# Causal masks, a bias and the hop scores brought into the score banks by 64x64 products

## The chip, the core and the metric

The kernel runs on one core of a Trainium2 chip. The metric is the device time of one execution in microseconds. A core has TensorE (PE, matrix products), VectorE (DVE), ScalarE (ACT), POOL and SyncE (SP, which issues DMA transfers). Each engine works through its own instructions in order, and semaphores tie them together. TensorE writes only to PSUM, which has banks of 512 fp32 columns on 128 partitions.

## The reference

Two decoder layers on x of 128 sequences x 64 positions x 128 features, each step with a residual and a LayerNorm behind it. Cut to the four attentions that the change touches and the places of the others:

```python
# layer 0
# attention: 16 heads of 8, causal; its output goes through a convolution
# that gives q2, and a second causal attention runs with q2 and the same k, v
scores = jnp.where(tril, einsum('bthd,bshd->bhts', q, k) * scale, -inf)   # twice
# "xattn": mLSTM with hop embeddings, 8 heads of 16
pe = rpe[hops].reshape(S, S, NH, DH)
k_hop = einsum('bhvc,vmhc->bhvm', qh, pe)
C = (einsum('bhsd,bhtd->bhst', qh, k_scaled) + k_hop) * D
# "ffn": rotary causal attention, 16 heads of 8, then 8 experts, top 2
scores = jnp.where(tril, einsum('bqhd,bkhd->bhqk', q, k) / sqrt(hd), -1e9)
# layer 1
# attention: rotary, grouped keys, causal
scores = jnp.where(tril, einsum('bshd,bthd->bhst', q, k) * scale, -inf)
# xattn: the last attention, with a bias per sequence
scores = einsum('bhnd,bhmd->bhnm', qh * scale, kh) + attn_bias[:, None] + attention_mask[:, None]
# ffn: 16 experts, top 2
```

## The kernel before, in words

A tile is two sequences of 64 positions, so 128 rows, and there are NT = 64 tiles. Five loops run over them or over expert slots. Each engine has its own program for each loop, with the order inside a period written out by hand; a period works on several tiles at different steps, and `live` cuts off those that don't exist at the ends. Waits are made by `after(engine, signals...)` and `wait_ge`.

- The first loop (lines around 800 to 842 on TensorE) has the first attention, its convolution and the second attention of layer 0. `scores1(0, i + 1, ...)` and `scores1(1, i - 1, ...)` write the scores of a tile for both.
- Then the hop table is made: k_hop for all sequences goes to DRAM (`hop_dram`), one row per sequence and position with 8 heads x 64 columns.
- The third loop (TensorE up to line 1016) has the mLSTM and the attention of the "ffn". Its order on TensorE ends with the hop scores (lines 1003 to 1016), its mask is `causal5(1)` followed at once by `scores5`.
- The experts of layer 0 follow; then the loop with both attentions of layer 1 (TensorE lines 1061 to 1139): `a5[0]` is the rotary one, with `causal5(0)` well ahead of its scores, and `a5[1]` the last one, with `bias5(1, fm[u])` ahead of its scores. `fm` is the sum of fside and mask, made by POOL (line 2104).
- The second routing, experts and final LayerNorm follow.

The scores of a tile for 16 heads fill two PSUM banks, `scores_ps[:, a, g, :]` with g = 0, 1 for the heads of a half. `a` picks the pair of banks. What is to be added to the scores (mask, bias, hop scores) is put in first by a product with the identity and start=True, and the scores are added to it with start=False. The product with the identity uses all 128 rows and columns of the array, the scores themselves 64x64 quarters: rows 64g for the heads' features, columns 64b for the sequence b. Softmax goes on with VectorE (`row_max`, then `probs` = scores less row_max, in halves), ScalarE (exp into probs), TensorE (`turn_half`, `turn5`: transposes), ScalarE (copy to `turned`), TensorE (`weigh`), VectorE (`recip`, `ctx_o`), TensorE (`turn_ctx`). POOL spreads the keys into a block form (`k_bd`, `shared`, both by a helper) and takes the power of -1/2 for the LayerNorms.

SyncE loads, in `load_hops`, the hop rows of a tile by one transfer into `hop_in`, and in `load_side` a tile of the context, of fside and of the mask by one transfer each. `c_loaded` counts them, 16 per transfer, and the waits on it are worked out from a count of 24 per tile.

Of the kernel before, what the change touches and what calls it, by code (L numbers as in the profile page):

```python
# [29 lines left out]
ALU = mybir.AluOpType  # L30
# [70 lines left out]
def build(nc, T, out):  # L101
# [6 lines left out]
    with ExitStack() as ctx:  # L108
# [141 lines left out]
        fm_in, fm = both("fm_in", 2 * S), both("fm", S)  # L250
# [202 lines left out]
        X4_LOADS, SIDE_LOADS = RING + PUT_LOADS + 16 * NT, RING + PUT_LOADS + 24 * NT  # L453
# [46 lines left out]
        def _(sp):  # L500
# [71 lines left out]
            def load_hops(n, u):  # L572
# [5 lines left out]
                sp.dma_start(hop_in[u], tile_rows(hop_dram, n)).then_inc(c_loaded[u], 16)  # L578
# [146 lines left out]
        def _(pe):  # L725
# [84 lines left out]
            def period(i, j):  # L810
# [12 lines left out]
                if live(i - 1):  # L823
                    after(pe, (q2_copied, i), (tr_copied[1], 2 * i - 2))
                    scores1(1, i - 1, q_T[1], (j - 1) % UN)
# [10 lines left out]
                if live(i + 1):  # L836
                    after(pe, (q1_copied, i + 2), (s["k_copied"], 2 * i + 4 + 4), (tr_copied[0], 2 * i + 2))
# [43 lines left out]
            def causal5(a):  # L881
                for g in range(NR):
                    pe.matmul(scores_ps[:, a, g, :], ident16, causal16.unsqueeze(1).broadcast_to([P, 8, S]),
                              start=True, stop=False, skip_group_check=True)

            def bias5(a, bias):
                for g in range(NR):
                    pe.matmul(scores_ps[:, a, g, :], ident, bias.unsqueeze(1).broadcast_to([P, 8, S]),
                              start=True, stop=False, skip_group_check=True)
# [41 lines left out]
            def period(i, j):  # L931
# [44 lines left out]
                if live(i - 1):  # L976
                    after(pe, a3.copied.of(i - 2))
                    causal5(1)
# [24 lines left out]
                if live(i + 2):  # L1003
                    after(pe, m_copied.of(i + 1), m_shift.of(i + 1), (c_loaded[u], RING + 24 * (i + 2 - u) + 48))
# [1185 lines left out]
```

## Time and profile before

| | us |
|---|---|
| median of 3 runs | 3979.63 |
| lowest, highest | 3977.45, 3980.4 |
| span of the profiled execution | 4030.4 |

The profile is of one execution; its span runs from the first to the last instruction, and is what the rows below refer to. Its views give, in microseconds, busy time by engine, waits by the instruction that waited and the one that released it, and the instructions in order of time.
### The profile page before, as it was taken

To read this page: it belongs to the slowest core of one execution; us is meant where nothing else is said; L and a number is where in the kernel's file an instruction comes from. 1 tells how busy PE (TensorE), PEld (TensorE's weight loads), DVE (VectorE), ACT (ScalarE), POOL (GpSimd) and SP (SyncE) were. 2 spreads that over 40 slices of the span, in tenths; PEclk is the share of its full clock that TensorE was granted. 3 is DMA by queue.
4 is the path that set the end of the run, shared out by engine and by line. 5 is a ranking of instruction groups with operands and counts; after the bars stand their busy time and mean duration, and the time that the engine had idled before them with its cause. 6 is when DMAs were issued, how large, how long until landed. Compare 5 with 4: busy or idle time off the path is not lost.

```text
span 4030.4 us, 92744 instructions
## 1 busy us (share of the span) xinstructions
PE 2840.4 (70%) x28014; PEld 1934.9 (48%) x28017; DVE 2454.1 (61%) x6828; ACT 1588.4 (39%) x3994; POOL 1864.3 (46%) x2306
## 2 busy tenths in 40 slices
PE   3999999758888888881068879999999920266600
PEld 2666666435555555551046656666666610255500
DVE  2777777528888887883011158888888860255445
ACT  2666666324555554540023335555555510011100
POOL 4222222006666666664720046666666617411177
PEclk9999999978999988985589989999999965699855
DMA  2111111351111111111222211111111102111133
GB/s 51 41 41 39 38 41 43 119 167 43 53 48 48 48 48 43 50 28 45 73 77 69 67 32 31 27 28 29 29 27 27 25 15 78 60 55 56 51 83 85
DMA packets 282376, 207.13 MB, mean 51 GB/s; under 512 B 61730, under 2 KB 246455, under 8 KB 281904
## 3 DMA queue, kind: packets, MB, share of 16 engines
q1 hardware_dynamic: 262960, 164.88, 13.9%
q0 software_dynamic: 19200, 39.62, 3.5%
q8 instruction: 105, 1.72, 0.2%
q14 instruction: 111, 0.91, 0.1%
HBM read 114.99 MB, written 90.18 MB: 51 GB/s over the span
## 4 chain that ended last, share of the span: by engine, by line
issue 22%; PE 14%; POOL 11%; DVE 5%; SPq 1%; DMA 0%; POOLq 0%; ACT 0%; DVEq 0%; another core or an unknown queue 0%; ACTq 0%
PE scores_ps L1047 3%; POOL k_bd L1999 2%; POOL shared L1999 2%; POOL got L2096 2%; POOL rows L2051 2%; PE heads_ps L1054 1%; PE desk_ps L1054 1%; PE scores_ps L1165 1%; POOL shared L2150 1%; POOL norm_rstd L1995 1%; PE scores_ps L1167 1%; PE heads_ps L1165 1%; PE desk_ps L1165 1%; DVE e_T L1819 1%; DVE row_max L1573 1%
## 5 line engine op out<-in xcount | busy, mean ns | idle before, releaser
L1995 POOL TENSOR_TENSOR norm_rstd<-norm_veps,minus_half 128x1 f32<-128x1 f32 x384 | 218.0, 568 | 386.3 <-DVE norm_veps L1555 380.6
L2051 POOL DMA_INDIRECT rows<-e_in,slot_put x256 | 249.1, 973 | 164.1 <-issue 107.4
L1276 ACT ACTIVATE probs<-probs 128x512 f32<-128x512 f32 x384 | 240.1, 625 | 132.2 <-DVE probs L1575 131.9
L1573 DVE TENSOR_REDUCE row_max<-scores_ps 128x8 f32<-128x512 f32 x384 | 262.1, 683 | 24.6 <-issue 14.1
L1280 ACT ACTIVATE turned<-scores_ps 128x512 f32<-128x512 f32 x384 | 228.4, 595 | 118.0 <-PE scores_ps L905 112.1
L1575 DVE TENSOR_TENSOR probs<-scores_ps,row_max 128x512 f32<-128x512 f32 x384 | 265.6, 692 | 13.3
L905 PE MATMUL scores_ps<-consts,probs 128*128 128x128 f32 x1536 | 243.7, 282 | 7.7 <-ACT probs L1276 6.8
L1208 ACT ACTIVATE probs<-probs 128x512 f32<-128x512 f32 x256 | 161.3, 630 | 136.1 <-DVE probs L1494 133.8
L1492 DVE TENSOR_REDUCE row_max<-scores_ps 128x8 f32<-128x512 f32 x256 | 174.9, 683 | 62.8 <-PE scores_ps L756 58.1
L2140 POOL TENSOR_TENSOR o_rstd<-o_veps,minus_half 128x2 f32<-128x2 f32 x72 | 50.0, 694 | 293.8 <-DVE o_veps L1924 284.1
L905 PEld LDWEIGHTS scores_ps<-consts,probs 128*128 128x128 f32 x1536 | 176.6, 144 | 16.6 <-ACT probs L1276 10.1
L1494 DVE TENSOR_TENSOR probs<-scores_ps,row_max 128x512 f32<-128x512 f32 x256 | 177.0, 691 | 8.8
L1987 POOL TENSOR_TENSOR shared<-k_raw,consts 128x1024 f32<-128x1024 f32 x32 | 60.7, 1898 | 241.3 <-issue 225.5
L1157 PE MATMUL turned_ps<-consts,shared 128*128 128x128 f32 x144 | 31.3, 304 | 196.3 <-issue 196.3
L1212 ACT ACTIVATE turned<-scores_ps 128x512 f32<-128x512 f32 x256 | 144.8, 596 | 61.3 <-PE scores_ps L765 61.3
L1987 POOL TENSOR_TENSOR k_bd<-k_raw,consts 128x1024 f32<-128x1024 f32 x32 | 60.7, 1898 | 232.5 <-issue 226.1
L1364 ACT ACTIVATE shared<-scores_ps,e_b 128x512 f32<-128x512 f32 x128 | 88.0, 687 | 197.3 <-PE scores_ps L1047 194.3
L1438 ACT ACTIVATE shared<-scores_ps,o_b,o_g 128x128 f32<-128x128 f32 x144 | 58.2, 454 | 269.7 <-PE scores_ps L1182 269.7
L765 PE MATMUL scores_ps<-consts,probs 128*128 128x128 f32 x1024 | 151.4, 280 | 15.9 <-ACT probs L1208 15.9
L2096 POOL DMA_INDIRECT got<-moe,got_at x128 | 127.7, 998 | 72.1 <-POOL got_at L2092 50.8
L1047 PE MATMUL scores_ps<-e_T,e_w 128*128 128x512 f32 x256 | 123.2, 626 | 42.9 <-DVE e_T L1819 41.9
L772 PE MATMUL turned_ps<-v_bd,turned 128*64 128x18 f32 x4096 | 144.8, 214 | 10.6 <-ACT turned L1212 2.7
(337 smaller groups left out, 8322.3 us busy)
## 6 DMA issues: line engine op xcount, KB each, us to landing
hop_dram<-shared SPq DMA_DIRECT2D x64, 256.0 KB, 2.1
hop_in<-hop_dram SPq DMA_DIRECT2D x64, 256.0 KB
rows<-zero_rows SPq DMA_DIRECT2D x64, 144.0 KB
shared<-rows SPq DMA_DIRECT2D x72, 128.0 KB
moe<-shared SPq DMA_DIRECT2D x72, 128.0 KB, 1.8
rows<-zero_rows SPq DMA_DIRECT2D x64, 128.0 KB
c_in<-in_ctx SPq DMA_DIRECT2D x128, 64.0 KB
c_two<-in_ctx SPq DMA_DIRECT2D x128, 64.0 KB
```

The costliest lines, as they stand in the source:

```text
L905: last = pe.transpose(scores_ps[:, a, g, P * k:P * k + P], probs[a][:, P * hp:P * hp + P], ident)
L1047: pe.matmul(scores_ps[:, f // 2, f % 2, 0:GS], e_w1[w][:, P * f:P * f + P], e_T[u], start=True, stop=True).then_inc(up_done, 1)
L1208: act.activation(half, half, ACT.Exp, scale=SCALE).then_inc(exp_ready[a], 1)
L1276: act.activation(half, half, ACT.Exp, scale=scale).then_inc(at.exped.sem, 1)
L1280: act.activation(turned[a][:, 512 * g:512 * g + 512], scores_ps[:, a, g, :], ACT.Identity)\
L1492: dve.tensor_reduce(best, sc, AX, ALU.max).then_inc(sub_ready[a], 1)
L1494: dve.tensor_tensor(probs[a][:, 512 * g:512 * g + 512].rearrange("p (h t) -> p h t", t=S), sc, best.unsqueeze(2).broadcast_to([P, 8, S]), ...
L1573: dve.tensor_reduce(best, sc, AX, ALU.max).then_inc(at.shift.sem, 1)
L1575: dve.tensor_tensor(probs[a][:, 512 * g:512 * g + 512].rearrange("p (h t) -> p h t", t=S), sc, best.unsqueeze(2).broadcast_to([P, 8, S]), ...
L1995: pool.tensor_tensor(n_rstd[:, k, u, :], n_veps[:, k, u, :], minus_half[:, 0:1], ALU.pow).then_inc(sig.sem, 1)
L2051: pool.indirect_dma_start(out=rows, out_offset=bass.IndirectOffsetOnAxis(ap=slot_put[:, c, U * n + i:U * n + i + 1], axis=0), in_=put_rows ...
L2096: pool.indirect_dma_start(out=got[u][:, D * k:D * k + D], out_offset=None, in_=moe0, in_offset=bass.IndirectOffsetOnAxis(ap=got_at[u][:, k ...
```

## The change

Mask, bias and hop scores now go in by 64x64 products too, one for each of the four quarters (g, b). Quarter g reads its rows of the identity and of the added values, so both halves of the partitions must hold the values of both sequences by query position: the mask constant already does, and the other two are loaded to suit. `hop_in` is loaded by two transfers (one for each half of the heads; rows of 64 positions, the two sequences side by side), and fside and mask are each loaded twice, once to either half of the partitions, so `fm_in` and `fm` are twice as wide and POOL adds 128 columns instead of 64. A tile now counts 32 on `c_loaded` for the hop loads and 40 for the side loads, and the constants of the waits follow. A wait on `zeroed` (reached early in the kernel) stands ahead of the quarters.

```diff
@@ buffers and counts
-        fm_in, fm = both("fm_in", 2 * S), both("fm", S)
+        fm_in, fm = both("fm_in", 2 * NB * S), both("fm", NB * S)
-        X4_LOADS, SIDE_LOADS = RING + PUT_LOADS + 16 * NT, RING + PUT_LOADS + 24 * NT
+        HOP_LOADS, FM_LOADS = 32, 40
+        X4_LOADS, SIDE_LOADS = RING + PUT_LOADS + 16 * NT, RING + PUT_LOADS + HOP_LOADS * NT
@@ SyncE, load_hops and load_side
-                sp.dma_start(hop_in[u], tile_rows(hop_dram, n)).then_inc(c_loaded[u], 16)
+                halves = tile_rows(hop_dram, n).rearrange("(b v) (g k) -> g v b k", b=NB, g=NR)
+                for g in range(NR):
+                    sp.dma_start(hop_in[u][64 * g:64 * g + 64].rearrange("p (b k) -> p b k", b=NB), halves[g])\
+                      .then_inc(c_loaded[u], 16)
-                sp.dma_start(fm_in[u][:, 0:S], tile_rows(fs_flat, n)).then_inc(c_loaded[u], 16)
-                sp.dma_start(fm_in[u][:, S:2 * S], tile_rows(mask_flat, n)).then_inc(c_loaded[u], 16)
+                for k, rows in enumerate((fs_flat, mask_flat)):
+                    by_query = tile_rows(rows, n).rearrange("(b v) m -> v b m", b=NB)
+                    for g in range(NR):
+                        sp.dma_start(fm_in[u][64 * g:64 * g + 64, P * k:P * k + P].rearrange("p (b m) -> p b m", b=NB), by_query)\
+                          .then_inc(c_loaded[u], 16)
@@ TensorE
+            def mask_quarters(a):
+                for g in range(NR):
+                    rows = slice(64 * g, 64 * g + 64)
+                    for b in range(NB):
+                        pe.matmul(scores_ps[S * b:S * b + S, a, g, :], ident16[rows, rows],
+                                  causal16[rows].unsqueeze(1).broadcast_to([64, 8, S]), start=True, stop=False,
+                                  skip_group_check=True)
             def scores1(a, n, q, k):
-                for g in range(NR):
-                    pe.matmul(scores_ps[:, a, g, :], ident16, causal16.unsqueeze(1).broadcast_to([P, 8, S]),
-                              start=True, stop=False, skip_group_check=True)
+                mask_quarters(a)
...
             def bias5(a, bias):
                 for g in range(NR):
-                    pe.matmul(scores_ps[:, a, g, :], ident, bias.unsqueeze(1).broadcast_to([P, 8, S]),
-                              start=True, stop=False, skip_group_check=True)
+                    rows = slice(64 * g, 64 * g + 64)
+                    for b in range(NB):
+                        pe.matmul(scores_ps[S * b:S * b + S, a, g, :], ident[rows, rows],
+                                  bias[rows, S * b:S * b + S].unsqueeze(1).broadcast_to([64, 8, S]),
+                                  start=True, stop=False, skip_group_check=True)
...
                     for g in range(NR):
-                        pe.matmul(scores_ps[:, 0, g, 0:256], ident, hop_in[u][:, 256 * g:256 * g + 256], start=True, stop=False,
-                                  skip_group_check=True)
+                        rows = slice(64 * g, 64 * g + 64)
+                        for b in range(NB):
+                            pe.matmul(scores_ps[S * b:S * b + S, 0, g, 0:256], ident[rows, rows],
+                                      hop_in[u][rows, 256 * b:256 * b + 256], start=True, stop=False, skip_group_check=True)
@@ POOL
-                    pool.tensor_tensor(fm[1 - u], fm_in[1 - u][:, 0:S], fm_in[1 - u][:, S:2 * S], ALU.add)\
+                    pool.tensor_tensor(fm[1 - u], fm_in[1 - u][:, 0:P], fm_in[1 - u][:, P:2 * P], ALU.add)\
                         .then_inc(fm_added.sem, 1)
```

`causal5` is gone; `mask_quarters` takes its place in both later loops.

## Rows read from the trace of the kernel before

**Rows 1.** The page: busy time (share of the span) and instructions by engine.

```profile
PE 2840.4 (70%) x28014; PEld 1934.9 (48%) x28017; DVE 2454.1 (61%) x6828; ACT 1588.4 (39%) x3994; POOL 1864.3 (46%) x2306
```

**Rows 2.** Windows: stretch, us; busy of PE, PEld, DVE, ACT, POOL; PEclk, DMA, GB/s.

```profile
60.00:720.00 660.00, 619.61 (x7720) 410.27 (x7720) 462.70 (x1059) 421.91 (x1007) 177.89 (x188) 0.99 0.13 39
...
1294.60:1307.70 13.10, 11.14 (x118) 7.35 (x118) 11.93 (x41) 6.53 (x18) 9.45 (x13) 1.00 0.20 53
1307.70:1322.30 14.60, 12.63 (x118) 7.63 (x117) 12.86 (x42) 8.15 (x21) 10.86 (x14) 0.88 0.16 48
...
1317.00:1320.40 3.40, 3.40 (x13) 0.95 (x14) 2.63 (x10) 2.18 (x5) 1.08 (x2) 0.53 0.20 57
...
2701.10:2715.00 13.90, 12.91 (x147) 9.03 (x147) 12.04 (x30) 7.75 (x21) 9.05 (x13) 1.00 0.11 28
```

**Rows 3.** Waits of TensorE, 60 to 720: total us, times, longest.

```profile
PE turned_ps L780 <- DVE ctx_o L1503: 14.5, 60, 0.3
```

**Rows 4.** Timeline of TensorE, stage 1: start, us, instruction, [idle before <- releaser].

```profile
299.91 0.59 PE L750 MATMUL scores_ps<-consts 128*128 128x512 bf16 x2
...
300.12 0.38 PE L750 MATMUL scores_ps<-consts 128*128 128x512 bf16 x1
...
300.43 1.09 PE L756 MATMUL scores_ps<-shared,q_ring 64*64 64x512 f32 x8
301.45 0.66 PE L765 MATMUL scores_ps<-consts,probs 128*128 128x128 f32 x4
...
307.78 0.33 PE L780 MATMUL turned_ps<-consts,ctx_o 128*128 128x128 f32 x1 [0.23 <-DVE ctx_o L1503]
...
310.25 0.59 PE L750 MATMUL scores_ps<-consts 128*128 128x512 bf16 x2
```

**Rows 5.** Timeline of VectorE in stage 1, and a hand-off to it at 78.74.

```profile
301.36 0.15 DVE L1478 TENSOR_SCALAR veps<-mv 128x1 f32<-128x1 f32 x1
301.59 0.69 DVE L1492 TENSOR_REDUCE row_max<-scores_ps 128x8 f32<-128x512 f32 x1
302.32 0.69 DVE L1494 TENSOR_TENSOR probs<-scores_ps,row_max 128x512 f32<-128x512 f32 x1
302.93 0.68 DVE L1492 TENSOR_REDUCE row_max<-scores_ps 128x8 f32<-128x512 f32 x1
...
78.74 1.09 PE L756 MATMUL scores_ps<-k_bd,q_T 64*64 64x512 f32 x8
...
79.90 0.69 DVE L1492 TENSOR_REDUCE row_max<-scores_ps 128x8 f32<-128x512 f32 x1 [3.27 <-PE scores_ps L756]
```

**Rows 6.** Timeline of VectorE, where its chain comes back from POOL.

```profile
306.83 0.40 DVE L1482 TENSOR_SCALAR x_out<-y,mv,rstd 128x128 f32<-128x128 f32 x1 [2.50 <-POOL rstd L1975]
```

**Rows 7.** Waits of VectorE, 985 to 1800.

```profile
DVE rope_c L1581 <- PE heads_ps L936: 24.0, 20, 3.2
```

**Rows 8.** Timeline of a long period in stage 2 and the start of the next.

```profile
1307.68 1.03 PE L1006 MATMUL scores_ps<-hop_in,consts 128*128 128x256 f32 x4
...
1308.64 0.66 PE L1013 MATMUL scores_ps<-k_bd,e_T 64*64 64x256 f32 x8
1309.24 1.16 PE L936 MATMUL heads_ps<-h_T,ffn_attn_w 128*128 128x128 f32 x8
...
1316.99 1.03 PE L883 MATMUL scores_ps<-consts 128*128 128x512 bf16 x2 [0.69 <-ACT turned L1280]
...
1325.05 0.42 DVE L1581 TENSOR_TENSOR rope_c<-heads_ps,consts 128x256 f32<-128x256 f32 x1 [0.88 <-PE heads_ps L936]
```

**Rows 9.** Timeline of TensorE in stage 3.

```profile
2701.11 1.94 PE L888 MATMUL scores_ps<-fm,consts 128*128 128x512 f32 x4
2702.89 0.39 PE L1083 MATMUL desk_ps<-h_T,c_w 128*128 128x128 f32 x2
...
2708.96 0.33 PE L1118 MATMUL heads_ps<-consts,g_diag 128*128 128x128 f32 x1 [0.60 <-DVE g_diag L1559]
```

**Rows 10.** Timeline of POOL and of SyncE's issues in stage 3.

```profile
2704.82 0.31 POOL L2104 TENSOR_TENSOR fm<-fm_in 128x64 f32<-128x64 f32 x1
...
2707.07 0.38 SPq L658 DMA_DIRECT2D fm_in<-in_mask_BxSxS_ff  x1
```

More of the change, by code:

```diff
@@ L823, in period @@
                 if live(i - 1):
-                    after(pe, (q2_copied, i), (tr_copied[1], 2 * i - 2))
+                    after(pe, (zeroed, U + 1), (q2_copied, i), (tr_copied[1], 2 * i - 2))
                     scores1(1, i - 1, q_T[1], (j - 1) % UN)
@@ L836, in period @@
                 if live(i + 1):
-                    after(pe, (q1_copied, i + 2), (s["k_copied"], 2 * i + 4 + 4), (tr_copied[0], 2 * i + 2))
+                    after(pe, (zeroed, U + 1), (q1_copied, i + 2), (s["k_copied"], 2 * i + 4 + 4), (tr_copied[0], 2 * i + 2))
                     scores1(0, i + 1, q_ring[:, 1 - u, :], (j + 1) % UN)
@@ L976, in period @@
                 if live(i - 1):
-                    after(pe, a3.copied.of(i - 2))
-                    causal5(1)
+                    after(pe, (zeroed, U + 1), a3.copied.of(i - 2))
+                    mask_quarters(1)
                     after(pe, (zeroed, U + 1), f_spread.of(i - 1))
@@ L1079, in period @@
                 if live(i):
-                    after(pe, fm_added.of(i), a5[1].copied.of(i - 1))
+                    after(pe, (zeroed, U + 1), fm_added.of(i), a5[1].copied.of(i - 1))
                     bias5(1, fm[u])
@@ L1097, in period @@
                 if live(i + 1):
[L1098 removed]
+                    after(pe, (c_loaded[1 - u], SIDE_LOADS + FM_LOADS * (i + 1 - (1 - u)) + 2 * FM_LOADS), b_q_copied.of(i), a_v_copied.of(i + 2), b_v_copied.of(i))
                     pe.transpose(desk_ps[:, P:2 * P], c_in[1 - u], ident).then_inc(c_turned.sem, 1)
@@ L1105, in period @@
                 if live(i + 2):
-                    after(pe, a5[0].copied.of(i + 1))
-                    causal5(0)
+                    after(pe, (zeroed, U + 1), a5[0].copied.of(i + 1))
+                    mask_quarters(0)
                 if live(i - 2):
@@ L1310, in period @@
                 if live(i + 1):
-                    after(act, m_weighed.of(i - 1), (c_loaded[1 - u], RING + 24 * (i + 1 - (1 - u)) + 48))
+                    after(act, m_weighed.of(i - 1), (c_loaded[1 - u], RING + HOP_LOADS * (i + 1 - (1 - u)) + 2 * HOP_LOADS))
                     mvv = m_vbd[1 - u].rearrange("p (g b h c) -> p g b h c", g=4, b=NB, h=2)
@@ L2102, in period @@
                 if live(i + 1):
-                    after(pool, (c_loaded[1 - u], SIDE_LOADS + 24 * (i + 1 - (1 - u)) + 48), a5[1].score.of(i - 1))
-                    pool.tensor_tensor(fm[1 - u], fm_in[1 - u][:, 0:S], fm_in[1 - u][:, S:2 * S], ALU.add)\
+                    after(pool, (c_loaded[1 - u], SIDE_LOADS + FM_LOADS * (i + 1 - (1 - u)) + 2 * FM_LOADS), a5[1].score.of(i - 1))
+                    pool.tensor_tensor(fm[1 - u], fm_in[1 - u][:, 0:P], fm_in[1 - u][:, P:2 * P], ALU.add)\
                         .then_inc(fm_added.sem, 1)
```

11 lines of the change are left out of this document (3 added, 8 removed).

## Prediction

> **What bounds the kernel now.** I read the page's first two parts first. TensorE is busy 70% of the span, more than any other engine [rows 1], and a change that shortens TensorE's work looks welcome. The share says nothing about who waits, so I then took the windows by stage. The edits lie in three stages, each a loop over the 64 tiles: the first two attentions (about 60 to 720 us), the hop attention with the third softmax attention (985 to 1800), and the last two attentions (2430 to 3200). TensorE is busy 94%, 85% to 87% and 93% of them; VectorE is busy 70% in the first, 91% in an ordinary period of the second, and 87% in the third [rows 2]. I call these stage 1, 2 and 3. A steady period is 10.34 us in stage 1, from one first mask to the next (299.91 to 310.25 [rows 4]), 13.1 in stage 2 and 13.9 in stage 3 [rows 2].
>
> In stage 1 the waits view shows TensorE idle in every period, 0.24 us for VectorE's ctx_o (60 times) [rows 3], and a second time for ScalarE's probs. An engine that waits in each period doesn't set the period alone; the question for each masked score is what stands right behind it. The stage has two masks per tile.
>
> The mask of the first attention starts at 299.91, its scores at 300.43, and the four quarters of the scores run to 301.45 [rows 4]. VectorE's row_max on them starts at 301.59. The instruction before it ended at 301.51, so the two seem to follow closely, but VectorE overlaps neighbours that don't depend on each other by 0.08: the row_max at 302.93 starts before the probs of 302.32 ends at 303.01 [rows 5]. This row_max could have started at 301.43. It waits 0.16 us for TensorE, and no wait is listed since the gap is so short. The row of 79.90, where VectorE had been idle for 3.27 us, confirms it: there row_max comes 1.16 us after the start of the scores (78.74), here too (300.43 to 301.59) [rows 5]. From this row_max a closed chain goes on: VectorE, ScalarE's exp and k_raw, POOL's k_bd and rstd, VectorE's x_out at 306.83 [rows 6], ctx_o, the other attention's row_max and probs, and ScalarE's exp, which TensorE awaits with the next first mask right behind it. So the first mask is on the path for 0.16 us.
>
> The mask of the second attention isn't. Its scores are finished when VectorE is still held up by POOL's rstd (it waits 2.50 us for it), and TensorE itself waits 0.23 at 307.78 for the ctx_o that follows [rows 4, 6].
>
> In stage 2 an ordinary period is VectorE's. It is busy 11.93 of 13.10 us in small instructions with gaps between, and its regular wait is one for POOL's norm_rstd, not for TensorE [rows 2]. But some periods are long: 14.6 us with a mean granted clock of 0.88, among neighbours of 13.1 at 1.00. In them the stretch at 1317 is at 0.53 [rows 2], so TensorE's clock is at its lower level of 1.2 GHz; ahead of it TensorE had had waits, the last of them 0.69 us, and mostly short products. The mask group then takes 1.03 us, against 0.59 for the same in stage 1 [rows 4, 8], and in the next period VectorE's rope_c waits 0.88 us for L936 [rows 8]. The waits view has 24.0 us of that kind in 20 places [rows 7]. There TensorE's work is on the path.
>
> In stage 3 TensorE waits 0.60 us for the g_diag that VectorE writes [rows 9]. From there the path is TensorE's, L1118 to L1131 in the listing, with VectorE waiting for it at both LayerNorm and rope, and then VectorE's again, with one copy in it that lasts until POOL's k_bd ends. Neither the bias (L888, 2701.11 [rows 9]) nor this stage's mask (L883) lies between L1118 and L1131.
>
> **The change part by part.**
>
> Masks, 256 in all (128 in stage 1, 64 each in stages 2 and 3). Two 128x512 bf16 products become four of 64x64 weights. The second product starts 0.21 us after the first, and the scores 0.31 after that [rows 4]: 0.10 of the 0.31 is the step from 128x128 to 64x64. The scores show that four quarters overlap: eight instructions of 512 fp32 columns take 1.02 us where one after the other would take four times 0.46 and more. So a mask of quarters, one 512-column product's 0.21 for each g with the two b side by side, takes 0.10 + 0.21 up to the second g, and with my allowance of 0.04 for what does not overlap quite, 0.35 in all, for 0.52: it saves 0.17. Bounds: 0.21 if the step is free, and a loss of 0.42 (0.10 + 4 x 0.21 - 0.52) if nothing overlaps. I take 0.17, from the nearest row, L756. In stage 1 the first mask pays the smaller of 0.17 and the room of 0.16: 61 steady periods x 0.16 = 9.8 us. The second mask pays nothing; TensorE's wait at L780 grows from 0.23 to 0.4, and the cover is POOL's and VectorE's chain.
>
> Hop scores, 64 pairs. Two 256-column fp32 products take 0.96 us (1307.68 to 1308.64); the quarters behind them with as many columns take 0.60 (L1013) [rows 8]. The step between the tilings is moved ahead, not added, so I take 0.54 and a saving of 0.42 (bounds 0.36 and 0.5). With the mask that is 0.59 us of TensorE per period in stage 2, in ordinary periods all of it cover for nothing. In long ones the wait of rope_c shrinks by 0.59, and by 0.17 more for a mask at the lower clock. If there stay as many, 20 x 0.6 to 0.75 is 12 to 15 us. But TensorE gets emptier in these periods too, and a low clock came after its emptiest part; the periods can meet it more often, each time at a lower price. The other end is therefore no gain. I take the middle, 6 us.
>
> Bias, 64 pairs of 512 fp32 columns: 2701.11 to 2702.89 is 1.78 us [rows 9]; quarters take 1.02 [rows 4] and one step in, 0.10, so 0.66 to 0.76 is saved. It is all in front of the wait at L1118, which grows from 0.60 to about 1.3 us. Worth nothing on the path; the stage's mask too, which sits between unlike tilings and saves at most 0.1. What is late next is g_diag, as before.
>
> A rule speaks against the change here. The two tilings cost 0.10 us at one change [rows 4]; the Trainium skill (TensorEngine Tiling (Array Packing), Tiling Modes, Key Properties) says that changing the tiling mode drains the array. In stages 1 and 2 the number of changes stays, in stage 3 bias and mask each get into and out of 64x64 between 128-row products. By the rule the stage's saving falls from 0.7 to 0.5; both disappear in the same wait.
>
> Loads and POOL. The hop load becomes two and the side loads five instead of three, with about 0.38 us of SyncE's queue each [rows 10]. Behind them are the loads of other tiles a period ahead and one store; with five transfers of 0.38 SyncE's queue has 1.9 of 13.9 us filled, and the tile is used a period later. The sum of fm grows from 64 to 128 columns; 64 take 0.31 [rows 10], 128 at most twice that, and POOL then waits for VectorE anyway: nothing. The extra wait on zeroed is met from the start and is issued while earlier products run: nothing to 0.05 per mask.
>
> Sum: 9.8 + 6 = 16 us. The profiled execution spans 4030.4 us and the median of the runs is 3979.63, so the profile is 1.3% slower than what is timed; the terms are per period and I carry them over as they are: 3979.6 - 16 = 3964.
>
> **The rivals.** (a) Nothing on the path: VectorE's own chain follows within 0.16 us in stage 1, and if the quarters save less than I read, or the low-clock stretches of stage 2 eat up their part, the result is within 8 us of 3979. For it: the margin is a tenth of a microsecond. Against: the hand-off of 1.16 us at 79.90 and 300.43. (b) Slower: the clock. With less in front, TensorE's wait ahead of L1118 [rows 9] doubles, and L1118 to L1131 behind it is all on the path. If the clock falls there as it does in stage 2, each fall costs about 1.5 us, as a long period of stage 2 does (14.6 less 13.1 [rows 2]). It decides above 16 falls in the 61 periods (16 x 1.5 is the forecast's 16 us and 8 more); one in three, as in stage 2, is 20 x 1.5 = 30 us, or 3994. Against: this stage runs at 1.00 throughout today, at 93% busy. The Trainium skill (TensorE: Matmul & The Clock Gate, Why this matters for your kernels) warns that gaps between bursts of products bring the low clock back. (c) Everything TensorE saves is paid: 128 x 0.17 + 64 x 0.59 + 64 x 0.75 = 107 us, 3873. Against: the waits of [rows 3, 9]. If stage 1 pays both masks and stage 2 its 15 us, it is about 3945. (d) The quarters don't overlap when they stream one constant: the masks lose 0.42 and the bias 1.7 us; stage 1 loses 61 x 0.42 = 26, stage 3 what its wait of 0.60 doesn't cover, 61 x 1.1 = 67, so about 4070. Against: the scores, same tiles.
>
> **How the numbers follow.** Forecast (3952 to 3971) 0.50; more gain, around 3945, 0.10, and (c) 0.02; (a) 0.23; (b) 0.12; (d) 0.03. Low 3940 leaves out (c) and some more; high 3991 leaves out (d) and the larger half of (b). A measurement of this kernel can tell about 0.2% (8 us) from no change. Faster by more: the forecast, the larger gains: 0.60. Within: 0.26. Slower: (b), (d): 0.14.
>
> **What would show it.** The period of stage 1 falls from 10.34 to 10.18, with the gap before the first row_max gone and TensorE's waits at L780 and L765 longer. The mask group takes 0.35 up to the scores. In stage 2 ordinary periods stay at 13.1 and long ones come down to about 13.9; their number shows whether the clock takes back the rest. In stage 3 the period stays at 13.9 with the wait at L1118 near 1.3 us and the clock at 1.00; if it is below 1.00 there, rival (b) is at work. The prediction is wrong in kind if stage 3 gets shorter: then the bias was on a path that I didn't see.

## The result, and the profile after

The changed kernel took 3995.2 us (median of 20 runs, 3984.2 to 4009.6) against 3980.5 us for the kernel before (20 runs): a ratio of 1.0033, 95% interval 1.0023 to 1.0043, so 13 us slower (9 to 17). The forecast was 3964, 16 us faster.

The page of the changed kernel, against [rows 1]: TensorE has 78 us less work, and every other engine the same or a little more.

```profile
PE 2762.1 (69%) x29038; PEld 1911.3 (48%) x29041; DVE 2457.5 (62%) x6828; ACT 1588.8 (40%) x3994; POOL 1871.8 (47%) x2306
```

The span of this profile, 3988.1 us, is shorter than the 4030.4 of the profile that the prediction read. To tell whether the change or the one profile is odd, the kernel before was profiled again (run before2, below). Its span was 3983.8, and its stages are the yardstick from here on. Windows of the three stages in before2 (stretch, us; busy of PE, PEld, DVE, ACT, POOL; PEclk, DMA, GB/s):

```profile
60.00:720.00 660.00, 621.19 (x7720) 411.92 (x7720) 462.89 (x1059) 421.86 (x1006) 177.53 (x188) 1.00 0.13 39
985.00:1800.00 815.00, 688.47 (x6618) 438.48 (x6616) 676.89 (x2202) 411.64 (x1076) 533.11 (x681) 0.93 0.16 46
2430.00:3200.00 770.00, 740.29 (x8382) 517.06 (x8381) 684.00 (x1656) 444.70 (x1205) 515.56 (x682) 1.00 0.11 29
```

The same windows in the changed kernel:

```profile
60.00:720.00 660.00, 598.05 (x8062) 416.79 (x8063) 463.76 (x1072) 424.75 (x1013) 178.59 (x190) 0.99 0.13 39
985.00:1800.00 815.00, 665.24 (x6971) 444.70 (x6970) 677.66 (x2193) 406.81 (x1067) 530.77 (x679) 0.89 0.16 46
2430.00:3200.00 770.00, 702.05 (x8544) 475.82 (x8545) 678.31 (x1626) 436.50 (x1183) 513.27 (x670) 0.99 0.13 33
```

What is to be seen: TensorE's granted clock went from 0.93 to 0.89 in stage 2 and is below 1.00 in stage 3. What the windows can't show are the lengths of the stages. I take them between the same VectorE instructions in every trace (VectorE has as many in each kernel), from the one that starts nearest 60 us in the profile shown of before to that nearest 720, and so on:

| profile | stage 1 | stage 2 | stage 3 | period of stages 1, 3 |
|---|---|---|---|---|
| before, the profile shown | 657.5 | 815.5 | 770.6 | 10.34, 13.90 |
| before2 | 657.9 | 816.0 | 742.4 | 10.34, 13.39 |
| the changed kernel | 649.9 | 813.4 | 757.9 | 10.20, 13.53 |

Stage 1 does what was forecast (two of its periods, of 11.47 us, are at a lower clock; masks1, below, has none and 647.7 us). Its mask and scores in the changed kernel, and VectorE behind them, against [rows 4, 5]:

```profile
295.46 0.41 PE L760 MATMUL scores_ps<-consts 64*64 64x512 bf16 x4
295.70 1.03 PE L770 MATMUL scores_ps<-shared,q_ring 64*64 64x512 f32 x8
...
296.81 0.15 DVE L1492 TENSOR_SCALAR veps<-mv 128x1 f32<-128x1 f32 x1
296.91 0.69 DVE L1506 TENSOR_REDUCE row_max<-scores_ps 128x8 f32<-128x512 f32 x1
```

The scores come 0.24 us after the mask instead of 0.52, and row_max starts 0.10 after the start of the veps before it, where it had been 0.23 (301.36, 301.59): VectorE no longer waits for TensorE there.

Stage 3 against before2: the period is 0.14 us longer, and five periods are longer still (four of 15.09 us, one near the end of 16.9 for 14.9). The cause of the 0.14 us is in these rows. POOL and VectorE in before2:

```profile
2702.50 1.89 POOL L1999 TENSOR_TENSOR k_bd<-rope_k,consts 128x1024 f32<-128x1024 f32 x1
2704.35 0.32 POOL L2104 TENSOR_TENSOR fm<-fm_in 128x64 f32<-128x64 f32 x1
...
2704.45 0.36 DVE L1849 SCALAR_TENSOR_TENSOR h_mid<-got,got_w,x_in 128x128 f32<-128x128 f32 x1
```

and in the changed kernel:

```profile
2628.65 1.89 POOL L2013 TENSOR_TENSOR k_bd<-rope_k,consts 128x1024 f32<-128x1024 f32 x1
2630.50 0.46 POOL L2118 TENSOR_TENSOR fm<-fm_in 128x128 f32<-128x128 f32 x1
...
2630.60 0.51 DVE L1863 SCALAR_TENSOR_TENSOR h_mid<-got,got_w,x_in 128x128 f32<-128x128 f32 x1
```

VectorE's h_mid starts 0.10 us into POOL's sum of fm and ends 0.14 after it (2704.81 for 2704.67), and with the wider sum it still ends 0.15 after it (2631.11 for 2630.96). The sum's extra 0.14 us is handed on in full, on the chain that the prediction had called VectorE's. The Trainium skill (SBUF — State Buffer, SBUF: two separate sides) has the rule: VectorE, in an operation with two SBUF inputs, and POOL, in one that reads SBUF, hold one pair of ports in turns, and the later one waits for the whole of the other's instruction. H_mid has the SBUF inputs got and x_in, and these rows agree.

The longer periods are the clock. Two windows in stage 3 of the changed kernel, one period each, and the second of the two at its slow place:

```profile
2602.50:2616.03 13.53, 12.34 (x154) 8.40 (x153) 12.13 (x29) 7.72 (x22) 9.20 (x12) 1.00 0.13 34
2616.03:2631.10 15.07, 13.88 (x154) 8.98 (x153) 11.96 (x29) 7.82 (x22) 9.20 (x12) 0.89 0.12 30
...
2620.00:2621.00 1.00, 1.00 (x6) 0.83 (x4) 1.00 (x3) 0.61 (x3) 0.21 (x2) 0.50 0.17 38
```

The timeline of TensorE there:

```profile
2619.69 0.47 PE L1132 MATMUL heads_ps<-consts,g_diag 128*128 128x128 f32 x1 [0.81 <-DVE g_diag L1573]
...
2621.16 1.99 PE L908 MATMUL scores_ps<-k_bd,q_ring 64*64 64x512 f32 x8
```

Right behind TensorE's wait of 0.81 us for g_diag the clock is at 1.2 GHz, and the scores take 1.99 us for 1.09. Such a period is 1.56 us longer than its neighbours. The wait alone doesn't tell where this happens: its median is 0.81 us over all the periods of the stage (0.11 in before2), and the clock falls in 5 of 56.

Stage 2 has the same in another proportion. Three neighbouring periods of before2:

```profile
1387.34:1401.76 14.42, 12.60 (x119) 7.72 (x116) 11.69 (x40) 6.72 (x19) 9.80 (x13) 0.88 0.15 47
1401.76:1414.97 13.21, 11.33 (x124) 7.54 (x124) 11.65 (x38) 6.33 (x17) 8.92 (x11) 1.00 0.18 52
1414.97:1428.11 13.14, 11.18 (x124) 7.39 (x118) 11.97 (x41) 6.53 (x18) 9.47 (x12) 1.00 0.18 52
```

and with the change in this stage (run no_stage3, below):

```profile
1399.60:1412.81 13.21, 11.24 (x135) 7.90 (x135) 11.64 (x37) 6.33 (x17) 9.10 (x12) 1.00 0.18 52
1412.81:1426.67 13.86, 11.10 (x114) 7.06 (x114) 12.41 (x42) 6.65 (x19) 9.66 (x13) 0.88 0.17 49
1426.67:1440.54 13.87, 11.90 (x124) 7.70 (x126) 11.77 (x38) 9.02 (x22) 9.65 (x13) 0.88 0.16 49
```

One low-clock period in three has become two in three, each at about half the price: 40.77 us for three before, 40.94 after. The clock took back the whole gain of these periods. Other low stretches are longer. Before2 has three of 14 to 17 us, each at one of the loop's boundaries, which come every eighth period; the changed kernel has six of 10 to 17 us, and not only there. One begins shortly after 1704 and goes on well into the products behind the scores (windows of that period and of the stretch, and rows of TensorE's timeline):

```profile
1698.30:1714.03 15.73, 12.74 (x105) 8.11 (x105) 11.53 (x38) 9.15 (x21) 9.51 (x12) 0.71 0.12 35
1704.00:1714.50 10.50, 10.29 (x97) 7.03 (x97) 6.61 (x25) 5.47 (x11) 4.17 (x7) 0.54 0.09 26
```

```profile
1704.21 0.41 PE L760 MATMUL scores_ps<-consts 64*64 64x512 bf16 x4 [0.78 <-ACT turned L1294]
1704.42 1.49 PE L908 MATMUL scores_ps<-shared,q_ring 64*64 64x512 f32 x8
...
1711.92 2.07 PE L948 MATMUL heads_ps<-h_T,ffn_attn_w 128*128 128x128 f32 x8
```

L948 is what VectorE's rope_c waits for; at 2.07 us for 1.16 it is far from hidden. The period to which this belongs takes 15.7 us. In all TensorE was at 1.2 GHz for 164 us of stage 2 in the changed kernel and for 120 in before2.

### The profile page after: what moved, and what is told of

It reads as the page before. It is cut to its first block, busy times and chain, and to the rows that moved or that the text cites. A ratio compares the mean times of both kernels' runs of the same rounds, so it can differ in the third digit from the quotient of the medians.

```text
span 3988.1 us, 95448 instructions
## 1 busy us (share of the span) xinstructions
PE 2762.1 (69%) x29038; PEld 1911.3 (48%) x29041; DVE 2457.5 (62%) x6828; ACT 1588.8 (40%) x3994; POOL 1871.8 (47%) x2306
## 3 DMA queue, kind: packets, MB, share of 16 engines
q1 hardware_dynamic: 290608, 169.09, 14.4%
## 4 chain that ended last, share of the span: by engine, by line
issue 21%; PE 14%; POOL 13%; DVE 5%; POOLq 0%; DMA 0%; ACT 0%; DVEq 0%; ACTq 0%; SPq 0%
PE scores_ps L1061 3%; POOL rows L2065 2%; POOL k_bd L2013 2%; POOL shared L2164 2%; POOL shared L2013 2%; POOL got L2110 2%; PE heads_ps L1068 1%; PE desk_ps L1068 1%; PE scores_ps L1179 1%; PE scores_ps L1181 1%; POOL norm_rstd L2009 1%; PE desk_ps L1179 1%; DVE e_T L1833 1%; PE heads_ps L1179 1%; DVE row_max L1587 1%
## 5 line engine op out<-in xcount | busy, mean ns | idle before, releaser
L760 PE MATMUL scores_ps<-consts 64*64 64x512 bf16 x1024 | 112.5, 426 | 86.1 <-ACT turned L1294 49.0
```

## The experiments

Fourteen kernels ran, each timed against the kernel before. I divided the change by stage, then stage 3 and stage 2 by what could cost time there. The cuts of code leave out the wait on `zeroed` ahead of the quarters, and that the counts of loads have names.

### Is the profile shown typical? (before2)

No edit.

> The kernel before, unchanged, for a second profile beside the one whose span (4030.4 us) is 50 us over its own median of 3980. Theory A: the 50 us of the shown profile lie in stretches that the change doesn't touch (routing and experts, after 3200 us), so the second profile spans about 3980, its stage 1 has periods of 10.34 us, its stage 3 periods of 13.90. Theory B: the shown profile was unlike a timed execution in the attention stages themselves; then one of the three stages is shorter here by 20 us or more. The time itself: ratio 1.000.

Measured: ratio 0.9993 (0.9980 to 1.0006). Theory B is right for stage 3: 742.4 us for 770.6, a period of 13.39 for 13.90. The eight other profiles of kernels in which stage 3 keeps its loads and its sum as in before have 13.39 or 13.40 too. The rows tell where the half microsecond was. In the profile shown:

```profile
2725.24 1.06 PE L1131 MATMUL heads_ps<-x_T,l_w 128*128 128x128 f32 x8
...
2726.84 0.42 DVE L1581 TENSOR_TENSOR rope_c<-heads_ps,consts 128x256 f32<-128x256 f32 x1 [0.53 <-PE heads_ps L1131]
```

and in before2:

```profile
2710.87 1.06 PE L1131 MATMUL heads_ps<-x_T,l_w 128*128 128x128 f32 x8
...
2711.96 0.42 DVE L1581 TENSOR_TENSOR rope_c<-heads_ps,consts 128x256 f32<-128x256 f32 x1
```

Rope_c starts 1.60 us after the same products in the one and 1.09 in the other. Why is open; the products themselves look alike. It matters for the reading: the 0.60 us of [rows 9], TensorE's wait for g_diag, has a median of 0.11 us in before2, which is without this delay, so the change met a stage 3 with less slack than I thought.

### Stage by stage (masks1, stage2, stage3)

masks1 is the kernel before with one edit:

```diff
             def scores1(a, n, q, k):
-                for g in range(NR):
-                    pe.matmul(scores_ps[:, a, g, :], ident16, causal16.unsqueeze(1).broadcast_to([P, 8, S]),
-                              start=True, stop=False, skip_group_check=True)
+                mask_quarters(a)
```

> Before, with only the masks of the first two attentions as quarters. Theory A (a first mask on the path): 9 us faster than before, 3971, period of stage 1 10.20 for 10.34. Rival: the timed executions don't show it, because something that is fixed by the program's size or by the clock takes it back; then it is within 3 us of before, or slower.

Measured: 0.9976 (0.9965 to 0.9987), 10 us faster, a period of 10.20 to 10.21, the stage 647.7 us for 657.9. The part of the prediction on stage 1 stands.

stage2 has `mask_quarters(1)`, the quarters of the hop scores and their two loads, and everything else as before.

> Before, with only the hop scores, their two loads and the mask of the third softmax attention as quarters. Theory A (forecast): 0 to 15 us faster, about 6. Rival C, the clock in this stage: TensorE, with 0.6 us less to do in a period, is granted the lower clock more often; slower than before by 10 us or more, with a mean period of the stage above that of before and a lower granted clock. If the whole of the measured loss of 13 us comes from here beside gains of 9 us in stage 1, this kernel is over 20 us slower than before.

Measured: 1.0044 (1.0028 to 1.0060), 17 us slower. In its profile stage 2 is 826.3 us for 816.0, and the mean clock from 985 to 1750 us is 0.89; before2 has 0.93:

```profile
985.00:1750.00 765.00, 623.88 (x6479) 418.46 (x6480) 628.35 (x2043) 383.54 (x1007) 496.72 (x636) 0.89 0.16 47
...
1178.70:1195.00 16.30, 13.65 (x114) 8.51 (x113) 12.38 (x41) 6.73 (x19) 9.82 (x13) 0.69 0.15 43
```

Rival C, as far as the time and the clock go. Of its periods, 13 are over 15.2 us (8 in before2). Two of them, 16.3 us at a clock of 0.69 (the second row is one), lie where before2 has none.

stage3 has the bias, its loads and sum, and `mask_quarters(0)`, the rest as before.

> Before, with only the bias, its loads and sum, and the mask of layer 1's first attention as quarters. The profile of the changed kernel has stage 3 at a period of 13.53 us for 13.90, with four periods longer by 1.56. Theory A: the stage is faster in timed runs too, 0.37 x 61 less 4 x 1.56, so 13 to 16 us faster than before. Rival B (the clock falls in this stage): about 12 falls or more in a timed execution, no gain or a loss.

Measured: 1.0044 (1.0027 to 1.0062), 17 us slower; the stage 759.8 us for 742.4, a period of 13.53, five periods of 15.09, and one near the stage's end of 16.92 where before2 has 14.91. The clock falls in those five and once more by the last. Theory A took 13.90 as the period of before; against 13.39 there is no gain. In the stretch measured the sum of it is about 56 x 0.14 = 7.8 us, 5 x 1.56 = 7.8 and 2.0, together 17.6 for the 17.4 measured. Rival B had the kind right and not the number: under half of its 12 falls, since half of the loss isn't the clock's.

### Stage 3: the sum (sum_wide, stage3_moved)

sum_wide is before with

```diff
-                    pool.tensor_tensor(fm[1 - u], fm_in[1 - u][:, 0:S], fm_in[1 - u][:, S:2 * S], ALU.add)\
+                    pool.tensor_tensor(fm[1 - u].rearrange("p (b m) -> p b m", b=2), fm_in[1 - u][:, 0:S].unsqueeze(1).broadcast_to([P, 2, S]),
+                                       fm_in[1 - u][:, S:2 * S].unsqueeze(1).broadcast_to([P, 2, S]), ALU.add)\
```

> Before, with one edit: POOL's sum of fm writes 128 columns instead of 64 (the same values twice); loads, bias and masks as in before. Theory S: the period of stage 3 is 13.53 for 13.39, 61 x 0.14 = 8.5 us slower than before, no place at the lower clock in this stage. Rival: no difference, and the period of 13.53 is due to the quarters or to the loads.

Measured: 1.0029 (1.0017 to 1.0041); the stage is 751.9 us, 9.5 over before2, with a period of 13.53 and the one of 16.9 near the end. One operation of POOL, 64 columns wider, is worth the 0.14 us in every period and that late period's 2.0, with nothing else of the change there. The expectation missed in one point, though: it had no place at the lower clock, and there is one, by that late period. The stretch in sum_wide, then the same in before2:

```profile
3092.10:3107.10 15.00, 13.02 (x139) 8.79 (x137) 12.01 (x29) 6.79 (x20) 8.83 (x12) 0.89 0.12 26
```

```profile
3081.00:3094.40 13.40, 11.81 (x142) 8.29 (x140) 12.05 (x30) 7.13 (x21) 9.06 (x13) 1.00 0.12 29
```

So about 1.5 us of the 2.0, and of the 9.5, are a fall of the clock that came with the wider sum, though all of TensorE's work was in place.

stage3_moved is stage3 with the sum behind the first norm_rstd:

```diff
                 if live(i + 1):
-                    after(pool, (c_loaded[1 - u], ...), a5[1].score.of(i - 1))
-                    pool.tensor_tensor(fm[1 - u], ...).then_inc(fm_added.sem, 1)
-                if live(i + 3):
                     after(pool, norms[0].of(i + 3, norms[0].per - 1))
                     rstd5(norm_rstd[0], 0, 1 - u)
+                if live(i + 1):
+                    after(pool, (c_loaded[1 - u], ...), a5[1].score.of(i - 1))
+                    pool.tensor_tensor(fm[1 - u], ...).then_inc(fm_added.sem, 1)
```

> Kernel stage3, with POOL's sum of fm behind the first norm_rstd of its period, in POOL's idle time, instead of behind k_bd. In stage3 the sum of 128 columns takes 0.46 us for 0.32, VectorE's h_mid beside it ends only when the sum has ended (0.51 for 0.36), and the period is 13.53 for 13.39. Theory S (the sum is what holds h_mid): the period is 13.39 or less, down to 13.2 since h_mid no longer waits for a sum at all; the falls of the clock stay (6 places, 1.5 us each), so 6 to 12 us slower than before, or less. Rival (the longer period comes from the loads or from TensorE): 13.53 stays.

Measured: 1.0035 (1.0022 to 1.0048). The period is 13.38, and h_mid takes 0.35 us with no sum beside it:

```profile
2709.76 0.35 DVE L1865 SCALAR_TENSOR_TENSOR h_mid<-got,got_w,x_in 128x128 f32<-128x128 f32 x1
...
2711.89 0.45 POOL L2123 TENSOR_TENSOR fm<-fm_in 128x128 f32<-128x128 f32 x1
```

So the sum's price is gone. The late period is back at 14.9. But beside it there are now eight of about 15.0 us where stage3 had five, and the stage is 755.8 us: 13.4 over before2, and 8 x 1.6 = 12.8. TensorE was granted 1.2 GHz in each of the eight, and once more at the very start of the stretch. What is left is the clock.

### Stage 3: whose missing work (mask3, stage3_fill)

mask3 is before with `mask_quarters(0)` for `causal5(0)`.

> Before, with only the mask of layer 1's first attention as quarters (stage 3). It tells whose missing work makes the clock fall there. The bias keeps its 1.78 us and POOL's sum its 64 columns, so the period stays at 13.39. If the 0.2 us that the mask saves just ahead of the wait for g_diag is what lets the clock fall: several periods of 15 us, 5 to 12 us slower than before. If the bias is: none, within 4 us of before.

Measured: 1.0012 (1.0000 to 1.0025), stage 3 at 742.7 us and 13.40, no new long period. The mask alone doesn't bring the clock down (granted 1.00 over the whole stage); it is the bias's missing 0.76 us, alone or with the mask's. The timed runs are 5 us above before, at the edge of their interval, and the stage doesn't show them.

stage3_fill is stage3_moved with one line:

```diff
+                    causal5(0)
                     mask_quarters(0)
```

> Kernel stage3_moved (period 13.38 us, nine periods of 15.0 with a short stretch at the lower clock in them), with one edit: ahead of the quarters of the mask of layer 1's first attention its two 128x128 products are issued too, into the same banks, which the quarters then overwrite; half a microsecond of TensorE work in front of the wait for g_diag. Theory T (the clock falls because TensorE is emptier there): no or hardly any stretch at the lower clock in stage 3, period 13.38 throughout, stage 3 as long as in before (742 us), the whole kernel within 4 us of before: more work, and about 12 us faster than stage3_moved. Rival (the falls come with the tilings or with the loads): 6 to 9 falls stay, and the kernel is no faster than stage3_moved.

Measured: 0.9997 (0.9984 to 1.0010), against 1.0035 for stage3_moved: more work on TensorE made it 15 us faster. The clock from 2440 to 3170 us, first in stage3_moved, then in stage3_fill:

```profile
2440.00:3170.00 730.00, 672.82 (x8138) 454.58 (x8134) 639.85 (x1555) 415.34 (x1124) 492.09 (x645) 0.98 0.13 34
```

```profile
2440.00:3170.00 730.00, 701.34 (x8387) 463.13 (x8379) 652.05 (x1577) 422.53 (x1144) 500.83 (x652) 1.00 0.13 34
```

The stage is 741.7 us long, the same as before2 within 0.7, with every load, quarter and the wide sum of the change in it. TensorE's wait for g_diag is back at 0.12 us, and no place of the stage is at the lower clock. So the change's own loss in stage 3 is two things, and nothing over a microsecond is left for a third: the sum beside h_mid, and TensorE's clock.

### Stage 2: parts and a remedy (hops, mask2, no_stage3, stage2_fill)

hops has the quarters of the hop scores and their two loads alone, mask2 the mask of the third softmax attention alone.

> Before, with only the hop scores as quarters and their two loads; the masks stay 128x128. Kernel stage2 (hop scores and that stage's mask) was 0.44% slower than before, 17 us. Theory T (TensorE's clock falls more often, and at dearer places, when this stage's periods hold less work): the 0.42 us that go out of each period here carry most of it, so 8 to 17 us slower, with stretches at the lower clock in over 12 places of the stage for 9 in before. Rival L (the second hop load, or its wait): slower by as much with the count of stretches as before. Rival M (the mask): this kernel is within 4 us of before.

> Before, with only the mask of the third softmax attention as quarters (stage 2). Theory T: 0.17 us less for TensorE in a period; 0 to 6 us slower, few more stretches at the lower clock. Rival M (this mask, which in long periods runs at the lower clock on the path): it carries the loss of kernel stage2, over 10 us slower. Forecast of the prediction: 1 to 3 us faster, since the mask in a long period is shorter.

Measured: hops 0.9994 (0.9983 to 1.0004), mask2 1.0008 (0.9995 to 1.0020). Neither costs by itself what the two cost together, 1.0044. Theory T missed in hops, where it had expected 8 to 17 us. Rival L falls as well: the second load is there, and no net cost over 2 us is. Rival M had hops right and mask2 wrong: the mask alone costs 3 us (up to 8 by its interval) and not over 10. The clock in stage 2, first hops, then mask2:

```profile
985.00:1750.00 765.00, 636.61 (x6489) 403.55 (x6488) 638.85 (x2081) 389.27 (x1022) 505.94 (x647) 0.92 0.17 48
```

```profile
985.00:1750.00 765.00, 637.67 (x6393) 428.20 (x6393) 639.16 (x2084) 390.13 (x1021) 506.91 (x647) 0.93 0.17 48
```

The record of the granted clock gives the count. TensorE was at 1.2 GHz in 33 stretches of stage 2 in hops, 140 us in all, and in 26 stretches and 113 us in mask2; the eight profiles with that stage as before have 22 to 27 stretches and 96 to 126 us (before2 25; the 9 of the expectation were counted otherwise, from the spacing of instructions). So in hops the clock does fall more often, as Theory T had it, and it costs nothing, because each fall costs less: such periods take 14.12 us where before2 has 14.54. With hop scores and mask together (stage2, no_stage3 and the changed kernel) there are 164 to 206 us, and six or seven stretches of 10 us or more where the other profiles have one to four.

no_stage3 is the changed kernel with stage 3 undone.

> The changed kernel with stage 3 as it was before (bias, its loads and sum, and that stage's mask undone). If the parts add up: the changed kernel (1.0033) less stage 3 (0.0044) gives 0.999 of before, and masks1 with stage2 0.9976 + 0.0044 = 1.002; so between 3976 and 3988. Stage 3 itself: period 13.39, one long period as in before.

Measured: 0.9999 (0.9987 to 1.0010). Against masks1 the stage-2 part costs 0.23%, 9 us (3 to 16, by the two intervals). Its stage 2 is 824.6 us, with the lowest clock of all:

```profile
985.00:1750.00 765.00, 635.28 (x6500) 420.00 (x6500) 633.84 (x2053) 384.93 (x1010) 500.82 (x638) 0.88 0.16 48
```

One profile says little on this stage, though: the eight profiles with the stage-2 code of before have 805.5 to 819.0 us, since the long periods fall differently in each. The timed runs are the better witness, and they put the stage-2 part at 9 us (no_stage3 against masks1) to 17 (stage2).

stage2_fill is the kernel before with four products that nobody uses:

```diff
+            def fill(n, k):
+                after(pe, a3.copied.of(n, 1))
+                for _ in range(k):
+                    pe.matmul(scores_ps[:, 1, 0, :], ident16, causal16.unsqueeze(1).broadcast_to([P, 8, S]),
+                              start=True, stop=True, skip_group_check=True)
...
+                if live(i - 1):
+                    fill(i - 2, 1)
                 if live(i + 7):
                     after(pe, xc_copied.of(i + 7))
...
+                    fill(i - 2, 3)
                     after(pe, a3.copied.of(i - 2))
                     causal5(1)
```

> Before, with one edit: in stage 2 four products of 128x512 bf16 that nobody uses are issued into the first bank of the third softmax attention while it is free, one ahead of the wait for xc_copied (0.42 us) and three ahead of the wait for the last turned half (0.69 us); the mask then overwrites the bank. Theory T: TensorE's clock stays up in ordinary periods, the 14 to 16 periods of 14.5 us become 13.13, so stage 2 is shorter by some 20 us and the kernel 3960 to 3965. Rival 1 (the falls don't depend on what TensorE does there): their count stays, same time as before. Rival 2 (the fills delay what waits for TensorE): slower by up to 10 us, periods over 13.2.

Measured: 0.9904 (0.9886 to 0.9921), 38 us faster, more than Theory T had expected. Stage 2 takes 781.0 us. Of the periods beside the loop's boundaries (which keep 16 to 17 us every eighth) nearly all are 13.13 to 13.4. Two stretches at 1.2 GHz are left, 27 us in all, for 25 and 120 us in before2. Its clock, and its TensorE where the waits had been:

```profile
985.00:1750.00 765.00, 686.42 (x6720) 439.64 (x6718) 657.74 (x2158) 403.43 (x1058) 525.41 (x669) 0.98 0.17 49
```

```profile
1296.93 0.38 PE L752 MATMUL scores_ps<-consts 128*128 128x512 bf16 x1
1297.52 0.40 PE L985 MATMUL turned_ps<-gate_w,e_T 128*128 128x16 f32 x2 [0.21 <-ACT e_out L1340]
...
1299.01 0.81 PE L752 MATMUL scores_ps<-consts 128*128 128x512 bf16 x3
1299.86 0.60 PE L899 MATMUL scores_ps<-consts 128*128 128x512 bf16 x2
1300.40 1.09 PE L912 MATMUL scores_ps<-shared,q_ring 64*64 64x512 f32 x8
```

The wait of 0.69 us ahead of the mask [rows 8] is filled, and the mask takes 0.60 and the scores 1.09 in every ordinary period.

### The whole change with the clock kept up (mended, best_a)

mended is the changed kernel with the edits of stage2_fill, stage3_moved and stage3_fill. best_a is before with the edits of masks1 and stage2_fill, nothing else.

> The changed kernel whole (all masks, hop scores and bias as quarters, all its loads), with the three edits that put back what it lost: the four filling products of stage2_fill in stage 2, POOL's sum behind the first norm_rstd, and the filling products of stage3_fill in stage 3. Theory T (the change's own loss is TensorE's clock in stages 2 and 3, and the sum beside h_mid): 9.5 us from stage 1 and 38 from stage 2's clock, nothing from stage 3: 3930 to 3940. Rival E (the hop scores' missing 0.4 us make stage 2 too empty even with the four products): stretches at the lower clock remain in stage 2, 10 to 25 us less of the gain, 3940 to 3960. Rival K (something else in the quarters or loads of stage 2 costs time): stage 2 is longer than in stage2_fill with no more low-clock stretches than there.

> Before, with the masks of stage 1 as quarters and the four filling products in stage 2; nothing else of the change. If the two effects add: 3980 - 9.5 - 38 = 3932 to 3935, ratio 0.988. Against mended it tells whether anything of the change beside stage 1's masks is worth having once the clock is kept up: mended within 4 us of this says no.

Measured: mended 0.9919 (0.9904 to 0.9935), 3948 us; best_a 0.9884 (0.9866 to 0.9903), 3932 us, 46 us faster than before: the two gains add up. Mended is 16 us behind, Rival E: its stage 2 is 795.0 us for 778.4 in best_a, with nine periods of 14.4 to 15.0 us (best_a has one such), and the same 13.13 for the rest. The clocks, mended first, then best_a:

```profile
985.00:1750.00 765.00, 654.58 (x6985) 431.72 (x6983) 646.06 (x2115) 394.63 (x1034) 513.90 (x657) 0.95 0.17 48
```

```profile
985.00:1750.00 765.00, 686.40 (x6772) 440.28 (x6771) 659.27 (x2165) 403.32 (x1056) 523.38 (x669) 0.98 0.17 48
```

Rival K falls, since mended does have more low-clock time. That the quarters of the hop scores and the mask lower the clock in stage 2 by making TensorE's part shorter is the likely reading, and stage3_fill is the case for it in stage 3. It isn't shown for stage 2: no run there keeps the quarters and their loads and gives back just the work that they took. Best_a, the version to keep, has 53 us more of TensorE work (2814.7 us) than the changed kernel.

## Why the prediction was wrong, point by point

**What bounds the kernel.** Right for stage 1: the first mask was on the path for the gap ahead of row_max, and nothing shows the second there (TensorE's wait at the ctx_o products grew from 0.24 to 0.55 us, forecast 0.4). Right for stage 2 in that VectorE's chain sets ordinary periods and the low clock the long ones. For stage 3 the place of TensorE's path was right (the clock's falls hit it at 1.56 us each), but the remark on the copy that lasts until k_bd ends was not followed one instruction further: h_mid behind it is held by POOL's next operation.

**Masks.** Priced at 0.35 us for 0.52; they took 0.24 up to the scores. The 0.46 us of a single product in the argument on overlap was too small: by [rows 9] an fp32 product of 512 columns takes 0.89 us, which only makes that argument stronger. What could be paid was the 0.16 of room, and 0.14 came: 10.20 for 10.34, 10 us in timed runs for the 9.8 forecast.

**Hop scores and the mask in stage 2: the first step that failed.** The work that leaves TensorE was priced at 0.59 us per period; by the medians of the changed kernel it is 0.81 (hop scores 0.48 for 0.96, the mask 0.21 for 0.54). More than that, the price of the clock was wrong. I wrote that the periods could meet the low clock more often, each time at a lower price, and then set "no gain" as the other end. Both halves happened: two periods in three for one, 0.72 us for 1.28 (13.86 and 14.42 less 13.14). That alone came to nothing. But the bound was wrong: nothing had excluded that the clock stays low for longer, as far as L948, and there it costs 2.6 to 3.2 us a period and not 1.3. The term was -6 us; the runs show +9 to +17.

**Bias: the term at nothing that wasn't.** It saves the 0.76 us that were forecast at most (1.02 for 1.78), and they are worth nothing on the path, as forecast. But they are not free: with them missing the clock fell at five places more in stage3 (four in the changed kernel's profile), about 8 us. That is rival (b), with its place, its price (1.5 forecast, 1.56 measured) and the sign right. Its number was wrong: it was to decide above 16 falls. The 3994 us it gave is near the 3995 measured by chance only; the loss has three parts of which it is one.

**Loads and POOL: the second step that failed.** "The sum of fm ... POOL then waits for VectorE anyway: nothing." The cover was looked for behind POOL's instruction and not beside it. It cost 9.5 us, by sum_wide's stage, about 1.5 of them through the clock. The loads themselves cost nothing that can be seen: stage3_fill has them and is level with before.

**The sum.** Term by term: stage 1 -10 for -9.8; stage 2 +9 to +17 for -6; stage 3 +17 for 0 (sum 9.5, clock 8). That is 16 to 24 us slower where the whole is 13 (9 to 17); the low end fits, and the parts don't add up better than their intervals.

**The rivals and the range.** Low clock in stage 2 stood in the text as what eats a gain, nowhere as a loss of its own, and so the range ended at 3991. With a loss in stage 2 as large as the gain of up to 15 us that was counted there, the range would have ended at 4006 and held the time. (c) and (d) found no support: TensorE's waits grew, and quarters do overlap. The Trainium skill's rule on changes of tiling mode wasn't seen to matter: in stage 3, where they are added, the mask takes 0.34 us for 0.44, and with all of them in place stage3_fill is level with before. The chances by outcome (0.60, 0.26, 0.14) aren't quite the sums of those in the list (0.62, 0.23, 0.15).

**The profile.** It was 1.3% over the timed median, and I carried its terms over unchanged. Three fifths of the excess over before2 (28 of 47 us) lay in stage 3, in one delay per period that later profiles don't have, and with it the slack of 0.60 us that I counted as cover.

**Open.** Why the profile shown had that delay; why hops and mask2 cost nothing or little alone and 0.44% together (the clock's record shows that there is more low-clock time, not why it sets in where it does); whether in stage 2 the missing work alone brings it, or the loads have a part; whether the bias alone, without the mask, brings the falls of stage 3.

## What to carry to other kernels

Where TensorE isn't on the path, taking work from it gains nothing and can lose: look in the windows for periods at a lower granted clock, and at what is behind them on the path, before making its products cheaper. There the remedy can go the other way: unused products in front of its waits, in a bank that is free then, took 38 us from the kernel before. And an operation whose own engine has time afterwards isn't free: look at what the other engines run beside it, and whether they end when it ends. Last, parts that cost nothing one by one can cost together, so time the whole as well.

## What the runs showed of the hardware that I had not expected

- How exactly VectorE's operation follows the end of POOL's beside it: h_mid took 0.36 us beside a POOL sum of 0.32, 0.51 beside one of 0.46, and 0.35 with none beside it. The short sum had happened to cost nothing.
- TensorE's clock answered to half a microsecond of work in a period of 13.4 us: granted 0.98 without (stage3_moved) and 1.00 with it (stage3_fill). In stage 2, four bf16 products of 0.21 us each moved it from 0.93 to 0.98.
- When the clock is low, it can be so for a few products (1.99 us for scores of 1.09) or over most of a period (1704.0 to 1714.5 at 0.54); a period of the second kind was longer by 2.6 to 3.2 us, one of the first by 0.7 to 1.6. More stretches needn't cost more: 33 for 25 in hops, at the same time as before.
- Four quarters of a 512-column bf16 product let the next group start after 0.24 us; two full-array products took 0.52.
